# Top-two routing by max and max-index, its weights on the GpSimd engine, and the weight splitting moved around it

## The reference

```python
x = x + xattn(layernorm(x), ctx, ...)      # two softmax maps of 16 heads, their weighted difference, RMS norm, projection
# feed-forward part, on h = layernorm(x), 2048 tokens:
probs = softmax(h @ gate_w.T)              # 2048 x 8
w, idx = top_k(probs, 2)
w = w / sum(w)
combine = zeros(T, E).at[arange(T)[:, None], idx].add(w)
for e in range(8):
    g, u = split(h @ gate_up[e].T)
    acc += combine[:, e:e+1] * (silu(g) * u @ down[e].T)
x = x + acc
```

## Time and profile before

| | us |
|---|---|
| median of the runs | 555.14 |
| the profiled execution | 548.71 |
| its span | 547.0 |
| TensorE busy in the span | 493.4 (90%) |
| VectorE busy | 385.6 (70%) |
| ScalarE busy | 343.0 (63%) |
| GpSimd busy | 278.7 (51%) |
| last gate product done | 224.2 |
| list of tokens done (`idx_ready`) | 246.3 |
| first expert matmul | 257.4 |

### The profile page before, as it was taken

How to read it: one execution, slowest core, us unless ns; L and a number is a source line. 1 busy time by engine, 2 the same in 40 slices (tenths; PEclk the granted TensorE clock), 3 DMA queues, 4 the chain that set the end, 5 groups by cost and what they waited for, 6 DMA issues and landing times.

```text
span 547.0 us, 12125 instructions
## 1 busy us (share of the span) xinstructions
PE 493.4 (90%) x3741; PEld 364.2 (67%) x3756; DVE 385.6 (70%) x797; ACT 343.0 (63%) x650; POOL 278.7 (51%) x356
## 2 busy tenths in 40 slices
PE   4795799999998988798998999999999999999991
PEld 3564466776665655345667987878888888777651
DVE  5770668998877857885877988876777667666551
ACT  2243678988888885574766776765656556545530
POOL 5442646556446453105226665666557555654244
PEclk9998799999999999799999999999999999999995
DMA  8558576876776534563657777866555457654224
GB/s 265 172 180 258 179 199 183 268 209 181 245 216 167 182 99 146 183 185 85 188 103 125 148 170 165 188 104 154 85 105 90 84 89 90 105 67 70 30 30 48
DMA packets 87882, 79.89 MB, mean 146 GB/s; under 512 B 48456, under 2 KB 73832, under 8 KB 87688
## 3 DMA queue, kind: packets, MB, share of 16 engines
q1 hardware_dynamic: 74300, 62.69, 41.5%
q0 software_dynamic: 11856, 16.16, 18.4%
q10 hardware_dynamic: 1668, 0.27, 0.3%
HBM read 49.08 MB, written 22.41 MB: 131 GB/s over the span
## 4 chain that ended last, share of the span: by engine, by line
PE 62%; DVE 10%; DMA 8%; ACT 6%; issue 5%; SPq 5%; POOL 1%; another core or an unknown queue 1%; ACTq 0%; DVEq 0%
PE bank L1551 26%; PE bank L1568 13%; PE bank L1349 4%; PE bank L1335 4%; SPq L489 3%; PE bank L1300 2%; PE bank L1580 2%; DMA q_parts<-WE 2%; PE bank L1372 2%; PE bank L1316 2%; PE bank L1358 2%; DVE FB L1223 2%; DVE FB L1227 2%; DMA WE<-x 2%; ACT FB L926 1%
## 5 line engine op out<-in xcount | busy, mean ns | idle before, releaser
L1551 PE MATMUL bank<-FB,WE 128*128 128x0 bf16 x1440 | 189.1, 282 | 1.1 <-DVE FB L1218 0.7
L1551 PEld LDWEIGHTS bank<-FB,WE 128*128 x1440 | 137.8, 98 | 33.2 <-issue 2.7
L728 POOL DMA_INDIRECT out<-FB,slot_tok x60 | 100.0, 1667 | 90.5 <-DVE FB L1244 84.5
L926 ACT ACTIVATE FB<-FB 128x512 bf16<-128x512 f32 x120 | 75.6, 630 | 70.2 <-DVE FB L1223 63.8
L1227 DVE TENSOR_TENSOR FB<-FB 128x512 bf16<-128x512 f32 x120 | 83.3, 694 | 47.2 <-ACT FB L926 41.9
L1568 PE MATMUL bank<-FB,WE 128*128 128x0 bf16 x720 | 103.8, 280 | 4.2 <-DVE FB L1227 2.1
L1223 DVE TENSOR_TENSOR FB<-FB,bank 128x512 f32<-128x512 f32 x120 | 81.9, 683 | 28.5 <-ACT FB L920 19.0
L719 POOL DMA_INDIRECT FB<-x_parts,slot_tok x60 | 61.7, 1028 | 69.4 <-DMA FB<-FB 27.9
L920 ACT ACTIVATE FB<-bank 128x512 f32<-128x512 f32 x120 | 70.6, 589 | 34.3 <-PE bank L1551 29.0
L1568 PEld LDWEIGHTS bank<-FB,WE 128*128 x720 | 67.7, 98 | 23.4 <-issue 7.7
L645 POOL TENSOR_TENSOR WE<-FB,WE 128x256 bf16<-128x256 f32 x104 | 67.8, 679 | 24.7 <-ACT WE L759 24.7
(11 more groups left out here) (186 smaller groups left out, 624.0 us busy)
## 6 DMA issues: line engine op xcount, KB each, us to landing
FB<-w SPq DMA_DIRECT2D x26, 512.0 KB, 5.2
WE<-w SPq DMA_DIRECT2D x44, 256.0 KB
WE<-q_parts SPq DMA_DIRECT2D x32, 200.0 KB
WE<-x SPq DMA_DIRECT2D x16, 256.0 KB, 5.7
q_parts<-FB SPq DMA_DIRECT2D x32, 128.0 KB
x_parts<-WE SPq DMA_DIRECT2D x20, 128.0 KB, 4.0
out<-WE SPq DMA_DIRECT2D x20, 128.0 KB, 5.1
q_parts<-WE SPq DMA_DIRECT2D x16, 128.0 KB
```

Of the source, the lines that this page charges most:

```text
L728: pool.indirect_dma_start(out=out, out_offset=bass.IndirectOffsetOnAxis(ap=slot_tok[:, c:c + 1].bitcast(U32), axis=0), in_=result_tile(c), ...
L926: nc.scalar.activation(hT[k % 3][:, 0, :], hid[k % 2], ACT.Copy).then_inc(hi_ready, 1)
L1551: ins = nc.tensor.matmul(to, wf[:, bass.ds(at + o, P)], xgT[s % 2][:, 2 * part + kc, :].shape_from_register(long[s % 2]), start=(z == 0), ...
```

## The change

- VectorE no longer copies the logits. For each tile, `max` writes the eight sorted values and, after a semaphore (`top_ready`), `max_index` writes their expert numbers, both from the PSUM bank; the second releases the bank. The two rounds over all tiles are gone. One comparison over both choices, 128 x (2 x 16 x 8), gives the one-hots, one addition the mask.
- The mask is laid out as it is written, tile by expert; TensorE reads it with a stride instead.
- The five instructions for the routing weights run on GpSimd, ahead of the gathers, with `pow` in place of `reciprocal`; VectorE waits for them (`parts_ready`) before it places the weights.
- The counting matmul uses a matrix of 0 and -1, so that one VectorE subtraction goes; the scan reads the PSUM bank, so that the copy goes.
- Both choices' slots are picked in one product and one reduction. Tile and place within it follow from three instructions instead of five, in numbers centred on 0 (MIDDLE).
- UNITS and FILL change: 10 units beside routing, none of them ahead of the mask's matmuls or of `turned_rows(0)`; FILL gets three more chunks in slot 1 and four in slot 6.
- `up(7, 0)` does not wait for `parked_in`; `down(7, 0)` does.
- A few constants are added on GpSimd and one table copy on VectorE.

```diff
-UNITS = (2, 10, 1, 1, 2, 1)
+UNITS = (0, 7, 1, 1, 0, 1)
-FILL = [... ((3, 4, 5, 6), (3,), (1, 3, 5, 6, 7), (1, 3, 5, 6, 7), (1, 2, 3, 5, 6, 7), (1, 2, 3, 5, 6, 7))) for c in chunks]
+FILL = [... ((3, 4, 5, 6), (1, 3, 5, 6), (1, 3, 5, 6, 7), (1, 3, 5, 6, 7), (1, 2, 3, 5, 6, 7), (1, 2, 3, 5, 6, 7), (1, 2, 3, 4))) for c in chunks]
...
+            pool.wait_ge(route_a, 1)
+            step(nc.gpsimd.tensor_scalar(r_sum, r_exp, 1.0, None, ALU.add))
+            step(nc.gpsimd.tensor_tensor(r_w[:, 0:TT], r_sum, r_minus, ALU.pow))
+            step(nc.gpsimd.tensor_tensor(r_w[:, TT:2 * TT], r_exp, r_w[:, 0:TT], ALU.mult))
+            step(nc.gpsimd.tensor_copy(r_wh, r_w))
+            nc.gpsimd.tensor_tensor(r_wl, r_w, r_wh, ALU.subtract).then_inc(parts_ready, 1)
             pool.wait_ge(idx_ready, 1)
...
-                        nc.vector.tensor_copy(r_cols, r_iota.unsqueeze(2).broadcast_to([P, P, JL]))
+                        nc.vector.tensor_copy(r_cols, r_iota[:, 0:NTP].unsqueeze(2).broadcast_to([P, NTP, JL]))
+                        nc.vector.tensor_copy(r_places, r_centred.unsqueeze(2).broadcast_to([P, P, JL]))
...
                     dve.wait_ge(lg_mm, n + 1)
-                    nc.vector.tensor_copy(logits[:, n, :], bank[bank_no("LG", n)][:, 0:E]).then_inc(lg_ready, 1)
+                    token_logits = bank[bank_no("LG", n)][:, 0:E]
+                    nc.vector.max(out=r_max[:, n, :], in_=token_logits).then_inc(top_ready, 1)
+                    dve.wait_ge(top_ready, n + 1)
+                    nc.vector.max_index(out=r_idx[:, n, :], in_max=r_max[:, n, :], in_values=token_logits).then_inc(lg_ready, 1)
...
-            (two rounds: L1116 to L1124, the mask L1127, the weights L1129 to L1134)
+            chosen = r_idx[:, :, 0:2].rearrange("p t c -> p c t").unsqueeze(3).broadcast_to([P, 2, TT, E])
+            step(nc.vector.tensor_tensor(r_oh, r_rank.unsqueeze(1).unsqueeze(1).broadcast_to([P, 2, TT, E]), chosen, ALU.is_equal))
+            nc.vector.tensor_tensor(r_mask, r_oh[:, 0], r_oh[:, 1], ALU.add).then_inc(route_m, 1)
+            nc.vector.tensor_tensor(r_diff, r_max[:, :, 1], r_max[:, :, 0], ALU.subtract).then_inc(route_d, 1)
 
             dve.wait_ge(route_mm, 1)
-            step(nc.vector.tensor_copy(flat(r_tot), bank[1][:, 0:P]))
-            step(nc.vector.tensor_tensor_scan(flat(r_inc), flat(r_reset), flat(r_tot), 0.0, ALU.mult, ALU.add))
-            step(nc.vector.tensor_tensor(flat(r_slot), flat(r_inc), flat(r_tot), ALU.subtract))
-            step(nc.vector.tensor_tensor(flat(r_slot), flat(r_slot), bank[0][:, 0:P], ALU.add))
+            step(nc.vector.tensor_tensor_scan(flat(r_inc), flat(r_reset), bank[1][:, 0:P], 0.0, ALU.mult, ALU.add))
+            step(nc.vector.tensor_tensor(flat(r_slot), flat(r_inc), bank[0][:, 0:P], ALU.add))
...
-            for c in range(2):
-                step(nc.vector.tensor_tensor(r_key, r_oh[c], r_slot.rearrange("p e t -> p t e"), ALU.mult))
-                step(nc.vector.tensor_reduce(r_sl[:, c * TT:(c + 1) * TT], r_key, AX.X, ALU.add))
-            step(nc.vector.tensor_copy(r_sli, r_sl))
-            step(nc.vector.tensor_single_scalar(r_tilei, r_sli, 7, ALU.arith_shift_right))
-            step(nc.vector.tensor_single_scalar(r_posi, r_sli, P - 1, ALU.bitwise_and))
+            step(nc.vector.tensor_tensor(r_key, r_oh, r_slot.rearrange("p e t -> p t e").unsqueeze(1).broadcast_to([P, 2, TT, E]), ALU.mult))
+            step(nc.vector.tensor_reduce(r_sl.rearrange("p (c t) -> p c t", c=2), r_key, AX.X, ALU.add))
+            step(nc.vector.tensor_scalar(r_tilei, r_sl, 1.0 / P, None, ALU.mult))
             step(nc.vector.tensor_copy(r_tile, halves(r_tilei)))
-            step(nc.vector.tensor_copy(r_pos, halves(r_posi)))
+            step(nc.vector.scalar_tensor_tensor(out=r_pos, in0=r_tile, scalar=-float(P), in1=halves(r_sl), op0=ALU.mult, op1=ALU.add))
...
+            dve.wait_ge(parts_ready, 1)
             for q in range(RG):
...
-            mask = r_mask.rearrange("p e t -> p (e t)")
+            mask = r_mask.rearrange("p t e -> p e t")
...
-                    if s == E - 1:
-                        pe.wait_ge(parked_in, 16)
...
                 pe.wait_ge(lo_ready, k + 1)
+                if s == E - 1 and c == 0:
+                    pe.wait_ge(parked_in, 16)
```

More of the change, by code:

```diff
@@ L172, in moe_attention_kernel @@
         sm = carver(FB[:, :], 1024)
-        r_mask = et(sm(TT * E, BF16))
-        r_m1, r_m2, r_top, r_diff, r_exp = (sm(TT) for _ in range(5))
-        r_w = sm(2 * TT)
+        r_mask = te(sm(TT * E, BF16))
+        r_diff, r_exp, r_sum, r_w = rt(TT), rt(TT), rt(TT), rt(2 * TT)
         r_wh, r_wl = rt(2 * TT, F16), rt(2 * TT, F16)
@@ L183, in moe_attention_kernel @@
         r_free = rt(NTP)
+        r_past, r_here, r_left = (rt(NS * E).rearrange("p (i e) -> p i e", e=E) for _ in range(3))
+        r_last = rt(E)
         r_exf, r_lenf = rt(NS), rt(NS)
-        r_past, r_here, r_left = (rt(NS * E).rearrange("p (i e) -> p i e", e=E) for _ in range(3))
         ffb = carver(FB[:, :], 13312)
@@ L288, in moe_attention_kernel @@
         lg_mm = sem("lg_mm")
+        top_ready = sem("top_ready")
         lg_ready = sem("lg_ready")
@@ L1481, in _, with slot_table, set_length @@
                     product(x2T_of(n), x2T_ready, n, gate_sb, E, lg_mm, bank_no(kind, n), lg_ready)
+            long = [nc.tensor.shape_register(n) for n in range(2)]
+            clamped = "the vector engine bounds the table by min and max before it stores it"
+            def slot_table():
+                _, v = nc.values_load_multi_w_load_instructions(slot_at[0:1, :], engines=[pe.engine], min_val=0, max_val=(E - 1) * EW,
+                                                                skip_runtime_bounds_check_because=clamped)
+                return v[0:NS], [nc.s_assert_within(n, 1, CAP, skip_runtime_bounds_check_because=clamped) for n in v[NS:2 * NS]]
+            def set_length(s):
+                pe.move_shape([long[s % 2]], [[(1, length[s])]])
             differences(UNITS[0])
             pe.wait_ge(route_m, 1)
-            mask = r_mask.rearrange("p e t -> p (e t)")
+            mask = r_mask.rearrange("p t e -> p e t")
             nc.tensor.matmul(bank[0][:, 0:P], r_before, mask, start=True, stop=True)
@@ L1507, in _ @@
             wf = WE[:, :, :].rearrange("p e n -> p (e n)")
-            long = [nc.tensor.shape_register(n) for n in range(2)]
             def turned_rows(i):
@@ L1516, in turned_rows @@
                 ins.then_inc(xgt_mm, 1)
-            clamped = "the vector engine bounds the table by min and max before it stores it"
-            def slot_table():
-                _, v = nc.values_load_multi_w_load_instructions(slot_at[0:1, :], engines=[pe.engine], min_val=0, max_val=(E - 1) * EW,
-                                                                skip_runtime_bounds_check_because=clamped)
-                return v[0:NS], [nc.s_assert_within(n, 1, CAP, skip_runtime_bounds_check_because=clamped) for n in v[NS:2 * NS]]
-            def set_length(s):
-                pe.move_shape([long[s % 2]], [[(1, length[s])]])
             def up(s, c, at):
```

64 lines of the change are left out of this document (27 added, 37 removed).

## The result

The changed kernel took 557.31 us (median of 20 runs, 552.2 to 562.7), the kernel before 553.75 us beside it (20 runs, 546.9 to 560.9): a ratio of 1.0087, 95% interval 1.0052 to 1.0122, so slower by some 4.8 us. (A ratio leaves disturbed runs out, so it can differ from that of the medians.) The prediction had 1 us less than before. Its profiled execution took 556.85 us, the span 555.0 us.

What follows compares the result with a forecast made beforehand. TensorE was taken to bound attention and longer expert slots, VectorE's instruction chain the routing between. Terms -6.5+0.7+0.45+0.2+2.9+1.3 = -0.95 us took 555.14 to 554.1 us, range 549.4 to 557.4.

Steps and rivals of the forecast that it cites:

- H: Entry to slot 7: two transposes queued behind the 1 MB load stall TensorE by 2.9 us (0.3 to 3.5).
- I: TensorE's low clock after the stall in slot 7: 1.3 us more (0 to 1.7).
- E: Token list to first expert matmul: two units gone, 1.7 of 2.17 us arrive; that matmul 6.5 us earlier in all.
- A to D: Routing, last logits to token list: fewer VectorE instructions bring the list 4.8 us earlier (bounds 4.0 and 5.5).
- Rival 3: Attention: VectorE's additions hold TensorE, 5.6 us arrive instead of 0.7; slower, 559.1 us; chance 0.10.
- Rival 4: Routing weights on GpSimd end late and delay the gathers: 2.9 us more, 557.0 us; chance 0.05.
- F: Attention: fourteen tiles cost VectorE 3.5 to 5.6 us more, of which 0.7 us arrives (0 to 2.5).
- G: Expert slots 1 and 6: late parts added to chunks cost 0.45 us in slot 1 and 0.2 in slot 6.
- Rival 1: Entry to slot 7: the transposes pass the 1 MB load, stall only 0.5 us; 550.5 us; chance 0.25.
- Rival 2: Entry to slot 7: the stall comes but TensorE's clock stays up; 552.9 us; chance 0.15.

Runs made afterwards that it cites:

- e_split_only: The kernel before with only the changed kernel's two lists of pieces (UNITS and FILL); median 11.2 us over the kernel before, ratio 1.028.
- e_weights_dve: The changed kernel with the five weight instructions back on VectorE, `reciprocal` for `pow`, ahead of the scan; 4.4 us over the kernel before, ratio 1.011.
- c_both: The changed kernel with the 1 MB load behind the two transposes and slot 6's late pieces in slots 2 to 5, second session; 5.9 us below before, ratio 0.988.
- e_before_max: The kernel before plus max, a wait and max-index in each tile, results unused, ahead of the logits copy; median +0.2 us, ratio 1.006.
- e_both: The changed kernel with the 1 MB load behind the two transposes and slot 6's late pieces in slots 2 to 5; 5.1 us below the kernel before, ratio 0.994.
- e_fill_early: The changed kernel with slot 6's late pieces moved to slots 2 to 5, queue order kept; median 1.8 us below the kernel before, ratio 1.005.

## Why the prediction was wrong, step by step

The forecast was 1 us less, the measurement 4.8 us more. Two terms of the sum had the wrong size: the two transposes behind the 1 MB load (H), with the low clock behind the stall (I), and the two pieces among the first transposes (E). They turn the sign of the stages; a further 2 to 5 us of the measured time lie outside of them and stay open.

*A to D, last logits to the token list.* Right. Last gate product to list: 17.2 us in all three profiles, 17.3 predicted. The top two took 0.48 (0.45), the compare 0.43 plus a step (0.48), and from the mask's end at 233.47 to the scan at 234.19 it was 0.72, with the matmuls at the low clock (0.59). The Trainium skill, "VectorE: DVE Perf Modes", section "Two Vector instructions with no wait between them", has it that finding an index is a pair of instructions. The trace agrees: MATCH_VALUE_LOAD 0.09 and FIND_INDEX8 0.17. Rival 3 took the bound of three operations, 0.9, for the nearer one for that reason; the three took 0.43 together, so a pair did not mean the higher price.

*E, list to the first expert matmul.* Too low: 10.15 to 10.2, predicted 9.3, before 11.05 and 10.8. The prediction named the gathers as what comes next once the pieces are gone. They are (0.33 us of idle time at 254.12), but the register load is later still: VectorE finishes the slot table at 255.53, 6.2 us behind the list (6.3 before), and the next transpose comes 2.9 us behind the table (3.0 in e_split_only), with TensorE idle for 2.22 of them. Before, there were 3.7 us between the two with 1.31 idle, so the pieces lay partly in time that the table needs anyway. The two pieces were worth 0.6 to 0.9 us, where the sum took 1.7. The first expert matmul so came 5.7 us earlier (33.0 to 27.3), 6.5 predicted, inside its bounds.

*GpSimd.* Right. `pow` on 16 columns took 2.93 us, a third of the upper bound, and all five instructions ended at 242.1, 7 us ahead of the list. Rival 4 falls; its price of 2.9 us was not worked out from any row. e_weights_dve shows why they had to move: the exponential ends at 237.54, 3.4 us after the scan began.

*F, attention.* Right that TensorE covers it: 119.6 to 121.0 us in the changed kernel beside 119.6 to 123.0, and no more idle time of TensorE than before. Nothing like 5.6 us arrived; rival 3 falls. The sum's +0.7 can't be told from zero.

*G, slots with extras.* Not seen. The part of the experts ahead of the entry to slot 7 has a mean of 118.0 us in both kernels, where 0.65 were to be added. Within the kernel before it varies by 2.0 us: each of its profiles has one idle time of TensorE of 1.3 to 1.8 us in an early slot, and the changed kernel's have none over 0.6. So 0.65 can't be told from zero.

*H, the entry to slot 7.* The mechanism was right, and the size of one term was the step that failed. The stall was 4.9 to 5.1 us, where the prediction took 2.9 and allowed 3.5. Counted from the first expert matmul, the late part ended at 116.3 (117.65 predicted) and the load landed at 122.2 (123.05), having needed 5.8 us (5.4 taken). Then the two transposes behind it took 3.8 us until the product began, 1.8 to 1.9 each in three profiles, where the sum had 1.75 for both and its upper bound 1.1 each. TensorE was also ready for slot 7 at 121.1, not 121.9. Why the transposes took twice as long is in part open: their packets ran among those of GpSimd's transfers, with a DMA share of 1.74 and only 99 GB/s moved, but no run keeps the order and takes GpSimd's transfers away.

That they stood behind the load, as the earlier trace rows suggested, is shown by c_both, where the load goes out at nearly the same time but behind the transposes and the wait is gone, and by the packets: the first began 4.0 us behind its issue, 1.2 where no load was in flight. The Trainium skill, "DMA: Bandwidth & Descriptors", section "Two DMAs through the same engine are not ordered", says that descriptors in one queue of one DMA engine start in order. The trace agrees. Rival 1, in which the transposes pass the load, falls by these runs.

*I, the clock.* It fell, as predicted, and cost more than its upper bound of 1.7 us. By the rows the twelve matmuls behind the stall took 2.78 us instead of 1.50, the six behind them 1.52 instead of 0.83 and the next twelve 1.64 instead of 1.50, together 2.1 us, where the sum had 1.3. This fits the entry as a whole: 7.1 us longer in the mean, of which 5.0 are the stall. H and I together so cost 7.1 us, with 4.2 in the sum. Rival 2 falls.

The sum of these: -5.7 in routing, 0.0 ahead of the entry, +7.1 at the entry and -0.3 behind it, +1.0 us instead of -1.65 (without the attention's 0.7). Routing erred by 0.8 and the entry by 2.9 to the slow side, G by 0.65 to the other. The prediction's balance stood on a difference of a gain of 6.5 and a loss of 4.85, and an error of 2.9 in the second is enough to turn its sign. That the measured median, 557.31, still lies below the upper end of the range, 557.4, is luck: that end was set by rival 4, which fell.

*What stays open.* The stages give +1.0 us, the runs +3 to +6, and against c_both on the same chip the stages give 4.9 of 9.0. In the profiles the rest lies ahead of the first gate product: 111.2, 112.9 and 112.3 in the changed kernel, 104.6, 112.3 and 104.2 in the kernel before, mean +5.1. Of this stretch the change touches only three more constants on GpSimd, and in four profiles of versions that have them it ended at 106.4, 106.6, 106.9 and 108.8, while in e_before_max, which lacks them, it ended at 112.1. e_both and c_both are one kernel, with 113.3 and 106.6. So both lengths occur with either set; whether the changed kernel falls into the longer one more often was not tried. One wait of TensorE for a transfer goes with the length: it was 7.1 to 8.8 us in all seven profiles whose first gate product came at 111.2 or later, and at most 5.1 in the other seven. In the changed kernel:

```profile
55.06 1.08 PE L1334 MATMUL bank<-WE 128*77 128x256 bf16 x4 [8.39 <-DMA WE<-WE]
```

## What to carry to other kernels

When a piece of work is moved later, follow the queue that its completion gates, not only the instruction that waits: here a load that nobody missed held two transposes behind it in SyncE's queue. Putting it behind them took 5.8 of the 7.1 us at the entry to slot 7 away, and with the late pieces moved as well the kernel came out 5.1 and 5.9 us under the kernel before. Take out the parts of a change one by one: the routing's change alone shortens the routing by 1.3 us, the split alone makes it 4.1 longer, and together they shorten it by 5.7, since each moves the others' wait (the mask behind pieces, the exponential behind a piece's lo part). Cut a stage at events around the place in question: the experts as a whole put 5.4 us down to the stall, the entry alone shows 7.1. When the forecast is a small difference of large terms, an error in one of them decides its sign, and the chances should say so.

## What the runs showed of the hardware

- Two DMA transposes issued 0.4 us and 1.7 us behind a 1 MB load on the same queue let the product that needed them begin 3.6 to 3.8 us after the load had landed; the first packet of the first began 4.0 us behind its issue, in e_fill_early, with no load in flight, 1.2 us. With the order reversed (c_both) all their packets had begun 1.9 us after the second issue, and the load took 7.7 us instead of 5.8.
- The packets of such a transpose are 512 of 256 bytes. Alone they took at most 0.05 us each (e_fill_early), among GpSimd's transfers up to 1.48 us (the changed kernel; DMA share 1.74, 99 GB/s).
- After 4.9 us without a matmul TensorE ran 12 matmuls in 2.78 us, with 1.50 before (granted clock 0.50), and was back at 1.00 some 4 us into its work.
- GpSimd's `pow` took 0.60 us on one column and 2.93 on 16.
- The span before the first gate product had lengths from 104.2 to 113.3 us over 14 profiles, with the same instructions in it but for three constants.
